# A transformer chain on one core: scales spread by TensorE, transfers split, a new written-out order, and 14 steps that multiply the identity with itself

## The reference, cut to what matters

```python
x = layernorm(x + attn0(x))   # 16 heads of 8; q and k by low-rank products; causal softmax
x = layernorm(x + ffn0(x))    # silu(x@w1*s1) * (x@w2*s2), gelu(.@h1*s3), gelu(.@h2*s4), .@w3*s5
x = layernorm(x + attn1(x))   # 16 heads of 8, full softmax
x = layernorm(x + ffn1(x))    # route each token to one of 8 LoRA experts on a shared 512-wide relu layer
```

## Time and profile before

| what | value |
|---|---|
| median of three runs | 828.52 us (827.58 to 831.6) |
| the profiled execution's own time | 828.5 us |
| its span, first to last instruction | 826.8 us |
| PE busy | 792.4 us (96%), 8626 matmuls |
| DVE, ACT, POOL busy | 619.0 us (75%), 412.1 us (50%), 186.3 us (23%) |
| mean granted TensorE clock | 0.974 |
| longest part of the chain that ended last | PE 79%, DMA 8%, DVE 5% |

### The profile page before, as it was taken

How to read it: one execution, slowest core, us unless ns; L and a number is a source line. 1 busy time by engine, 2 the same in 40 slices (tenths; PEclk the granted TensorE clock), 3 DMA queues, 4 the chain that set the end, 5 groups by cost and what they waited for, 6 DMA issues and landing times.

```text
span 826.8 us, 21566 instructions
## 1 busy us (share of the span) xinstructions
PE 792.4 (96%) x8626; PEld 610.8 (74%) x8626; DVE 619.0 (75%) x1749; ACT 412.1 (50%) x829; POOL 186.3 (23%) x397
## 2 busy tenths in 40 slices
PE   8879999999999999999999999999999999999796
PEld 6557777777778687887768777776878777786575
DVE  3666696886888697978779776788968776476775
ACT  1223517364744638374463646355393636636372
POOL 4221303031301313140222312130132303101022
PEclk9769999999999999999999999999999999999799
DMA  4652221304130314004050220304131110101200
GB/s 144 197 199 78 66 105 49 123 28 143 35 135 17 105 60 144 33 29 142 17 163 19 98 81 29 128 5 141 57 103 54 33 55 22 59 29 59 90 10 27
DMA packets 42572, 64.31 MB, mean 78 GB/s; under 512 B 5128, under 2 KB 33128, under 8 KB 42088
## 3 DMA queue, kind: packets, MB, share of 16 engines
q1 hardware_dynamic: 40696, 57.93, 21.5%
q10 hardware_dynamic: 1776, 5.00, 1.9%
HBM read 43.54 MB, written 18.35 MB: 75 GB/s over the span
## 4 chain that ended last, share of the span: by engine, by line
PE 79%; DMA 8%; DVE 5%; ACT 3%; SPq 2%; issue 2%; POOL 1%; POOLq 0%; DVEq 0%; ACTq 0%
PE banks L1128 26%; PE banks L1077 10%; PE banks L1044 6%; PE banks L988 6%; PE banks L1185 6%; PE banks L1110 6%; DMA krow<-scratch 5%; PE banks L955 3%; PE banks L1157 3%; DMA scratch<-split 2%; PE banks L1089 2%; PE banks L964 2%; ACT prob L622 2%; PE banks L1059 2%; PE banks L1052 2%
## 5 line engine op out<-in xcount | busy, mean ns | idle before, releaser
L745 DVE TENSOR_REDUCE top<-banks 128x3 f32<-128x384 f32 (+1 forms) x512 | 286.6, 613 | 50.5 <-PE banks L988 24.9
L622 ACT ACTIVATE prob<-banks 128x384 f32<-128x384 f32 (+1 forms) x512 | 242.5, 559 | 82.3 <-PE banks L1052 30.3
L636 ACT ACTIVATE hid<-banks 128x512 f32<-128x512 f32 x64 | 38.2, 597 | 211.8 <-PE banks L1128 211.6
L1077 PE MATMUL banks<-prob,v 128*32 128x256 f32 (+1 forms) x2048 | 117.9, 364 | 2.0 <-DVE low L875 1.2
L1128 PE MATMUL banks<-glu,wh 128*128 128x256 f32 x512 | 118.2, 384 | 0.1
L1128 PE MATMUL banks<-hid,wh 128*128 128x256 f32 x512 | 117.4, 382 | 0.2
L558 POOL TENSOR_TENSOR ln_rstd<-ln_var,minus_half 128x2 f32<-128x2 f32 x64 | 44.7, 702 | 320.7 <-DVE ln_var L824 320.4
L1128 PEld LDWEIGHTS banks<-glu,wh 128*128 128x128 f32 x512 | 94.8, 190 | 14.9 <-issue 1.1
L1128 PEld LDWEIGHTS banks<-hid,wh 128*128 128x128 f32 x512 | 94.8, 190 | 13.9 <-DVE top L745 1.2
L1077 PEld LDWEIGHTS banks<-prob,v 128*32 128x32 f32 x2048 | 58.9, 111 | 41.3 <-issue 10.0
L563 POOL TENSOR_TENSOR pool_carrier<-minus_half 128x1 f32<-128x1 f32 x128 | 25.3, 197 | 278.7 <-ACT prob L622 278.4
(11 more groups left out here) (113 smaller groups left out, 1024.9 us busy)
## 6 DMA issues: line engine op xcount, KB each, us to landing
scratch<-split SPq DMA_DIRECT2D x124, 128.0 KB, 2.2
qrow<-scratch SPq DMA_DIRECT2D x31, 512.0 KB, 3.8
krow<-scratch SPq DMA_DIRECT2D x62, 256.0 KB, 4.3
xt<-in_xt SPq DMA_DIRECT2D x16, 128.0 KB, 2.2
wh<-in_wh ACTq DMA_DIRECT2D x2, 1024.0 KB, 6.3
out<-xout SPq DMA_DIRECT2D x16, 128.0 KB, 2.1
x<-in_x SPq DMA_DIRECT2D x15, 128.0 KB, 2.3
prob<-in_qk_a SPq DMA_DIRECT2D x2, 512.0 KB, 5.4
```

Source lines behind the costliest of these rows:

```text
L622: nc.scalar.activation(prob[s][:, j % 2, g, 0:wide], banks[:, b, 0:wide], ACT.Exp, scale=1.0 / float(np.sqrt(np.float32(HD))) if s == A0 e ...
L636: nc.scalar.activation(hid[layer][:, 2 * m:2 * m + 2, :].rearrange("p m t -> p (m t)"), banks[:, g, :], ACT.Gelu).then_inc(gelued, 1)
L745: nc.vector.tensor_reduce(out=top[s][:, :, h], in_=banks[:, b, 0:blocks * wide].rearrange("p (q k) -> p q k", q=blocks), axis=AX, op=ALU.m ...
L1077: done = nc.tensor.matmul(banks[32 * i:32 * i + 32, g, q0:SEQ], v[s][:, kb, GROUP * j + i, :], prob[s][:, j % 2, i, kb * SEQ:(kb + 1) * SE ...
```

## The change

The scales are loaded into one partition only, 8 KB instead of 1 MB. PE gets three scale steps (letter v): it multiplies a row of ones with a row of scales, 512 columns, which spreads the scales over 128 partitions of a bank; v.0 has two such multiplies, v.1 and v.2 one each. DVE multiplies the weights with the bank. ACT's step late is in four parts instead of three: the two halves of wh are issued at two places of the order. All five strings are written anew, and BANK_TABLE with them; each letter occurs as often as before, apart from v and b on PE and x on ACT. PE has 14 steps b: b0 to b2 ahead of a2.0, b3 and b4 behind it, b5 and b6 between F15 and M15, b7 and b8 between N15 and O15, b9 to b13 between O15 and P15.

PE's new string begins with a0.0 d1 a0.1 c0 a0.2 e0 a0.3 v0.0 f0.0 g0 f0.1 a1.0 d2 a1.1 h0.0 h0.1 f0.2 a1.2 f0.3 a1.3 h0.2 c1 h0.3 g1 b0 b1 b2 a2.0 b3 b4 i0 f1.0 v0.1 f1.1 v0.2 j0 h1.0 f1.2 r0.0 r0.1. SP's begins with p0 p1 d1 p2 q1 d2 q2 g1 p3. On DVE e0 stands behind the tenth maximum of chunk 0, before behind the fourteenth. Between y15 and A15.0 PE's string had F12 A14.3 D13.2 D13.3 B14 M12 z14 E13 O11 N12 and has D13.0 C13.2 D13.1 A14.2 C13.3 D13.2 A14.3 N12 P11 D13.3 B14. Behind A15.0 it had C14.0 A15.1 C14.1 A15.2 D14.0 C14.2 D14.1 A15.3 and has O12 A15.1 z14 C14.0 C14.1 A15.2 D14.0 E13 C14.2 D14.1 A15.3.

```diff
@@ SEQUENCE "pe", first line and last lines
-        "adcaaadeffgahfhaafahhgaicffajhfrfhdrahhscasgaisasftfjdfhuchayzrfrahhsigAsaAsaAsAftBfjarCrufhyChDadfDCsgC"
+        "adacaeavfgfadahhfafahchgbbbabbifvfvjhfrrdhfsasahhasgcaisaftjfdauryarhfhgfshAhAsAisaAsafBtfcjazChhfuryCrf"
...
-        "rfNruChhfEyCOfsChDhDAsiCsjAsFArrtPADDsuzBMysCEsCsADtCDANCuAyFADDBMzEONACACADCDAPFCBOzMDDCPNCEDCDCFOMDDNP"
-        "EOFMPNOP"
+        "fBMtzfNcEPjCruCyfhhrfDDhCssAhssiOAtjCrADDruPsysAEsBFsMCztFNCAMOuAyDCDACDANPDBAOAzCCADECDAPCBFDMzDCNCEDCD"
+        "CFOMDDPNEOFbbMPNbbObbbbbP"
...
-            "scale": [(k,) for k in range(4)],
-            "late": [(k,) for k in range(3)],
+            "scale": [(k,) for k in range(4 if engine == "dve" else 3)],
+            "late": [(k,) for k in range(4)],
...
-                act.dma_start(early[:, HEADS * D:HEADS * D + 4 * HID], d_in["scales"].partition_broadcast(P)).then_inc(weights2, DMA)
+                act.dma_start(early[0:1, HEADS * D:HEADS * D + 4 * HID], d_in["scales"].unsqueeze(0)).then_inc(weights2, DMA)
                 act.dma_start(w12[:], d_in["w12"]).then_inc(weights2, DMA)
             elif k == 1:
-                for layer, there in enumerate((weights3, weights4)):
-                    act.dma_start(wh[:, layer], d_in["wh"][:, layer]).then_inc(there, DMA)
+                act.dma_start(wh[:, 0], d_in["wh"][:, 0]).then_inc(weights3, DMA)
+            elif k == 2:
+                act.dma_start(wh[:, 1], d_in["wh"][:, 1]).then_inc(weights4, DMA)
                 act.dma_start(w3raw, d_in["w3"]).then_inc(weights4, DMA)
...
-        def scale(s, n, k):
+        def scale(s, n, k, *bs):
+            if k < 3:
+                dve.wait_ge(scales_full, k + 2)
             if k == 0:
-                dve.wait_ge(weights1, NWEIGHTS1)
-                dve.wait_ge(weights2, NWEIGHTS2)
-                nc.vector.tensor_tensor(w12[:, 0, :], w12[:, 0, :], scales[:, 0, :], ALU.mult).then_inc(scaled_w, 1)
+                nc.vector.tensor_tensor(w12[:, 0, :], w12[:, 0, :], banks[:, bs[0], :], ALU.mult).then_inc(scaled_w, 1)
...
+        def scale(s, n, k, *bs):
+            pe.wait_ge(weights2, NWEIGHTS2)
+            pe.wait_ge(ones_made, 1)
+            for i, g in enumerate(bs):
+                at = 0 if k == 0 else k + 1
+                last.wait(pe, g)
+                nc.tensor.matmul(banks[:, g, :], ones[0:1, :].bitcast(F32), scales[:, at + i, :], start=True, stop=True).then_inc(scales_full, 1)
+                last.used(g, scaled_w, at + i + 1)
```

More of the change, by code:

```diff
@@ L64 @@
 CAUSAL = 2
-BARE = ('load', 'late', 'scale', 'keys', 'resid', 'fetch', 'norm', 'store', 'outputs')
+BARE = ('load', 'late', 'keys', 'resid', 'fetch', 'norm', 'store', 'outputs')
 KIND = {
@@ L185, in shared_banks @@
         elif step[0] not in BARE:
-            count = {"gated": 2, "expert": 2, "pass1": GROUP, "pass2": GROUP}.get(step[0], 1)
+            count = {"gated": 2, "expert": 2, "pass1": GROUP, "pass2": GROUP, "scale": 2 - (step[-1] > 0)}.get(step[0], 1)
             of[step] = [int(b) for b in BANK_TABLE[bank:bank + count]]
@@ L312, in build @@
         wqa = early[:, 0:HEADS * D].rearrange("p (n s d) -> p n s d", n=HEADS // 2, s=2)
-        scales = early[:, HEADS * D:HEADS * D + 4 * HID].rearrange("p (s o) -> p s o", s=4)
+        scales = early[0:1, HEADS * D:HEADS * D + 4 * HID].rearrange("p (s o) -> p s o", s=4)
         nothing = prob[A0][:, 0, 0, 0:P]
@@ L372, in build @@
         settled = {s: sem(f"settled{s}") for s in (A0, A1)}
+        scales_full = sem("scales_full")
         scaled_w = sem("scaled_w")
@@ L692, in _ @@
             last = Last()
-            def scale(s, n, k):
+            def scale(s, n, k, *bs):
+                if k < 3:
+                    dve.wait_ge(scales_full, k + 2)
                 if k == 0:
-                    dve.wait_ge(weights1, NWEIGHTS1)
-                    dve.wait_ge(weights2, NWEIGHTS2)
-                    nc.vector.tensor_tensor(w12[:, 0, :], w12[:, 0, :], scales[:, 0, :], ALU.mult).then_inc(scaled_w, 1)
-                    nc.vector.scalar_tensor_tensor(out=w12[:, 1, :], in0=w12[:, 1, :], scalar=0.5, in1=scales[:, 1, :],
+                    nc.vector.tensor_tensor(w12[:, 0, :], w12[:, 0, :], banks[:, bs[0], :], ALU.mult).then_inc(scaled_w, 1)
+                    nc.vector.scalar_tensor_tensor(out=w12[:, 1, :], in0=w12[:, 1, :], scalar=0.5, in1=banks[:, bs[1], :],
                                                    op0=ALU.mult, op1=ALU.mult).then_inc(scaled_w, 1)
                 elif k == 3:
+                    dve.wait_ge(weights1, NWEIGHTS1)
                     dve.wait_ge(weights4, 2 * DMA)
@@ L710, in scale @@
                         dve.wait_ge(weights4, 2 * DMA)
-                    nc.vector.tensor_tensor(wh[:, k - 1], wh[:, k - 1], scales[:, 1 + k, :].unsqueeze(1).to_broadcast([P, HB, HID]),
+                    nc.vector.tensor_tensor(wh[:, k - 1], wh[:, k - 1], banks[:, bs[0], :].unsqueeze(1).to_broadcast([P, HB, HID]),
                                             ALU.mult).then_inc(scaled_w, 1)
@@ L1188, in down @@
                 last.used(g, ln[s], 5 * n + 1)
-            walk(dict(warm=warm, qk=qk, v=v_, pass1=pass1, maxima=maxima, early=early, pass2=pass2, values=values, project=project, turn=turn, gated=gate, hidden=hidden, route=route,
+            walk(dict(warm=warm, scale=scale, qk=qk, v=v_, pass1=pass1, maxima=maxima, early=early, pass2=pass2, values=values, project=project, turn=turn, gated=gate, hidden=hidden, route=route,
                       lora=lora, expert=expert, down=down), "pe")
```

82 lines of the change are left out of this document (41 added, 41 removed).

## The result

| | before | change |
|---|---|---|
| median, 20 runs each on the same chip | 829.09 us (825.56 to 832.53) | 837.77 us (829.88 to 845.3) |
| ratio | | 1.0087, 95% interval 1.007 to 1.0105 |
| the profiled execution's own time, and its span | 828.5 and 826.8 us | 829.88 and 828.1 us |
| mean granted clock | 0.974 | 0.983 |

The change is slower. The medians are of all 20 runs, the ratio and its interval of the fast ones alone, without three of the change's that took over 842 us. The profiled execution of the change is the fastest of its 20.

What follows compares the result with a forecast made beforehand. The body was taken as bound by PE's work, its two ends by waits and the clock. Terms -5.5 +1.9 +1.0 -1.6 +0.5 -4.5 +3.2 = -5.0 gave span 821.8, time 823.5 us; range 815 to 833.

Steps and rivals of the forecast that it cites:

- the body: Between start and end, at most 9.3 us to win; PE work between producer and consumer much the same: +0.5 us.
- Start, waits (-5.5): Up to a2.0: smaller scales and earlier parking and fetches start a2.0 near 46 instead of 50.84: -5.5 us.
- Clock at the start (-1.6 behind a2.0): Behind a2.0: a fall still, but 10 us slow in place of 13.6: -1.6 us.
- Scale steps (+1.9): v0.0 runs while PE waits for DVE anyway; v0.1 and v0.2, in front of j0, add +1.9 us.
- Warm steps ahead of and behind a2.0 (0 and +1.0): At a2.0: b0 to b2 inside its wait cost 0; b3 and b4 behind it, where nothing is awaited, +1.0 us.
- End (-4.5): From y15 to the last A of chunk 15: shorter wait at A15.0, less loss, faster y15: together -4.5 us.
- last warm steps (+3.2): b5 to b13 before M15, O15 and P15, where the clock is already full, can only cost: +3.2 us.
- d2 behind a1.0: Slower rival at the start: a late a1.0 holds back chunk 2's projection and fetch; 836 us, chance 0.15.
- idle of the body above 14 us: Sign of being wrong: PE's idle in the body grows beyond 14 us.
- a clock that falls between 64 and 760 us: Sign of being wrong: the clock falls in the body, where it never fell before.

Runs made afterwards that it cites:

- g_start: The change's order on every engine up to the first down step, then the strings of the kernel before: 832.55 us, ratio 1.006.
- b_early1: Kernel before with only PE's A0.0 moved ahead of s1.0, i2 and g3: 836.40 us, ratio 1.0097.
- b_start: Kernel before with five warm steps at the start, three ahead of a2.0 and two behind it: 834.09 us, ratio 1.0063.
- b_ahead: Kernel before with only the three warm steps ahead of a2.0: 830.08 us, ratio 1.0016.
- b_spread: Kernel before with the scale steps on PE, the 8 KB scales and the split transfers, no warm steps: 834.10 us, ratio 1.0072.
- a_notail: The change without the nine warm steps of the end, b0 to b4 kept: 837.73 us, ratio 1.0092.
- a_nob: The change without all 14 warm steps: 831.84 us, ratio 1.0053.
- a_nobv: The change without all warm and all scale steps, with the 1 MB broadcast of the scales back: 840.75 us, ratio 1.0124.
- b_tail: Kernel before with the nine last warm steps at its end, at the change's places: 829.76 us, ratio 1.0014.
- a_again: The change unaltered, timed and profiled again: 838.91 us, ratio 1.0131.
- a_look4: The change unaltered, a fourth look, one profiled execution: 835.67 us.
- a_defer: The change with PE's first A step of nine chunks moved behind one to three following steps: 853.75 us, ratio 1.0306.
- a_spfix: The change with six letters of SP's string moved, parking and fetch of chunks 12 and 14 earlier: 844.04 us, ratio 1.0193.
- a_look3: The change unaltered, a third look, one profiled execution: 831.46 us.

## Why the prediction was wrong, by its steps

**The failed step is the body.** It stood in the sum with +0.5, bounds -3 and +5, as if its length did not depend on the start ahead of it. In the profiled executions the first to the last down step took 10.0 us more, with 6.2 more of idle in the body. g_start splits this. With the body strings of before behind the new start the stretch takes 7.1 us more, and the whole kernel is 3.9 us slower by the median (5.0 by the ratio), where the start's terms were booked as -4.2: so the larger part of the miss is a gain at the start that the body does not pass on. Body and end in their new orders, with the nine warm steps, were to give -0.8 (+0.5 -4.5 +3.2), and the change less g_start is +5.2. The prediction compared only how much PE work stands between a producer and its consumer and found it much the same (9.6 at chunk 0, 10.8 and more after). The runs showed two things that this count leaves out. First, the path from y or d to A or a runs through in-order queues of SP, ACT and DVE: 19 of the 24 us at a12.0 went by before SP issued the fetch, and moving six letters of SP's string moved a wait onto f11, of 5 us. Second, a wait costs more than itself when the clock falls behind it: 1.7 us more behind 1.28 us, 8.0 us in all for b_early1 with one of 4.15. The prediction itself read 10.8 us as what parking and fetch took at y15 and still took the tight chunks for free.

**The sum that the runs give instead.** By the medians the start with b0 to b4 is +3.9 (g_start) and body and end are +5.2, together 9.1 us, where 8.7 were measured. That the two add up is no test: they are differences of the same kernels, and only the chip differs. If b3 and b4 cost the +4 that b_start and b_ahead show, the rest of the start is about 0; no run has the start without them on the body of before.

**Start, waits (-5.5).** The first megabyte was indeed in the way: the wait for x is gone, also in b_spread, where d2 keeps its place (0.48 instead of 2.85 us), and a1.0 starts at 29.14. a2.0 starts 3.0 us earlier (47.80 against 50.84), not 5: the fetch took 8.2 us, though only one megabyte of wh was issued beside it. Up to the first down step the sum of the prediction's terms was -4.2, and -3.4 was measured: right in sum. But it is no gain of the whole: g_start, 2.2 us early at the first down step, is late at the last.

**Clock at the start (-1.6 behind a2.0).** Somewhat undersized. Behind a2.0 the clock is low for 8.5 us instead of 13.1 in the means, worth 2.3. Up to 80 us it is low 12.8 us less, which is worth half of that, 6.4 us. The Trainium skill (TensorE: Matmul & The Clock Gate, Terms) prices throttled time at its length times one minus the ratio, and that gives the same 6.4. It doesn't arrive in full even at the first down step. That the five warm and the scale steps take up to 6.3 us of work here, and that a part of the low stretch lay beside waits for DVE, would explain this; no run separates them.

**Scale steps (+1.9).** As said where they stand: no wait ahead of them in the change; their cost in time was not measured by itself. b_spread shows that at other places they would have waited 2.4 and 1.9 us for their banks, which the prediction did not count.

**Warm steps ahead of and behind a2.0 (0 and +1.0).** The three ahead are free (b_ahead 1.0016). The two behind are mis-sized: b_start less b_ahead says 4.0 us, the change less its five steps 3.3 to 5.9. In b_start they run at the low clock and so does all behind them up to 68 us. In the change they run at 2.4 GHz (1.16 us for both in all four executions), and the first down step comes no later with them but earlier: at 83.8 to 87.9 in the change and a_notail, at 89.4 and 89.2 in a_nob and a_nobv, which have none. So what they gain or cost by then is not what the medians show at the end; where it is lost isn't settled.

**End (-4.5) and last warm steps (+3.2).** In the change's trace A15.0 starts after 0.21 us of idle instead of 1.74, and the low clock of the end shrank from 13.7 to 3.4 us, but to 10.2 in the other three: in the means 8.5 instead of 11.3, worth 1.4, and A15.0's wait is gone there too or 0.34. So -4.5 was too much; what the end gives in all no run shows by itself. The warm steps cost less in the traces than the 3.2 said: from O14 to P15 it is 10.3 us before, 13.2 in the change, 11.1 in a_notail and 12.6 in b_tail, so the nine take 2.2 to 2.3, and 0.8 come with the new order (the wait of 0.95 for DVE in the rows below, 0.28 before). PE near the end of the change answers to the earlier trace rows:

```profile
815.40 0.44 PE L1161 MATMUL banks<-ident,low 128*128 128x128 f32 x2 [0.95 <-DVE low L878]
815.67 1.06 PE L945 MATMUL banks<-ident 128*128 128x128 f32 x8
...
818.78 2.39 PE L945 MATMUL banks<-ident 128*128 128x128 f32 x20
821.01 1.95 PE L1198 MATMUL banks<-wout,inter 128*128 128x128 f32 x16
```

P15 starts 2.23 us behind the first of the five. In the timed medians the nine steps are less than 1 us in b_tail and nothing in a_notail, less again.

**The rivals.** d2 behind a1.0 was priced at 836, close to the 837.8 measured, but by a mechanism that did not happen: a1.0 came earlier than forecast, not after 33. The prediction's own list named what did happen, as a sign of being wrong: idle of the body above 14 us (13.6 in the mean, 14.2 twice) and a clock that falls between 64 and 760 us.

**Open.** What in the new start makes the body of before take 7 us more (g_start), since an earlier first down step alone did not (b_tail); by what way b3 and b4 cost the change more than their work; when a wait of 1 to 2.5 us is followed by a fall of the clock; and the 3 us by which the medians differ more than the profiled executions. No version tried beats the kernel before.

## What to carry to other kernels

When all engines run written-out orders and one is busy 96% of the time, a new order is judged by the whole path from producer to consumer, queue by queue, not by the bottleneck's work between the two; moving one engine's step alone, ahead or back, made every order here slower. A gain at the start is not banked until the end: look at the time from the first to the last equal step too. Steps meant to keep TensorE warm were free ahead of a wait and worth nothing measurable (b_ahead); two of them behind it, 1.0 us of work, went with a loss of 4.0 (b_start).

## What was not expected of the hardware

One and the same stretch of instructions kept the clock at 2.4 GHz after 1.06 us of idle in one kernel (a_nob) and fell to 1.2 GHz after 1.28 us in another (a_nobv); the change itself, in four profiled executions, had 6.8, 6.8, 0 and 13.6 us of low clock in the body. The length of a wait tells little up to 2.5 us: in the body, over the profiled executions of all kernels here, 10 of the 68 waits of 1.0 to 1.5 us that began at full clock and 2 of the 13 of 1.5 to 2.5 us had a fall beside or right behind them, and all 7 of the longer ones. And the clock also fell where PE hardly waited. In a_again it did so at 174.0, where the waits just before are 0.40, 0.16 and 0.17 us. In a_look4, a_nobv, a_defer and a_spfix it fell at the same place; in the first profiled execution of the change, in a_look3, a_nob and a_notail it did not, with the same waits (0.40, 0.16 and 0.17 in a_nob). PE of a_again, with the longest wait ahead of this fall, the step in which the clock falls, and a longer wait without a fall:

```profile
171.89 0.38 PE L1047 MATMUL banks<-qrow,krow 32*128 32x256 f32 x4 [0.40 <-ACT prob L624]
...
173.91 1.45 PE L1080 MATMUL banks<-prob,v 128*32 128x256 f32 x16
...
484.99 0.50 PE L991 MATMUL banks<-krow,qrow 32*128 32x128 f32 x8 [2.33 <-DMA krow<-scratch]
```

The step at 173.91 takes 0.86 us in a_look3. So the low clock of the change's body can't all be put down to its longer waits for key rows. The orders with more waits of about a microsecond are also the more scattered ones, which is seen and not explained: the change's 20 runs span 15.4 us, those of the kernel before 7.0. The Trainium skill (TensorE: Matmul & The Clock Gate, What's actually happening) puts the ramp's penalty, the time until the clock is first granted in full, below 1% of a typical kernel span. The granted clock of 0.974 over 826.8 us is 21.5 us here, 2.6%; this is no measurement of the same thing, since most of it lies in later falls.
